# Expert weights fetched by SyncE at a row held in a register, instead of by a GpSimd gather

## What is computed

```python
logits = x @ router_w + router_b
topk_scores, topk_idx = top_k(logits, 2)          # 2 of 8 experts for each token
gates = softmax(topk_scores)
for e in range(8):                                # D_MODEL 256, D_FF 1024
    h = relu(x @ W1[e] + b1[e])
    y = h @ W2[e] + b2[e]
    out += y * combine[..., e]                    # the gate of expert e, 0 where it was not chosen
```

## Time and profile before

| | us |
|---|---|
| median of 3 runs | 1067.77 (1062.13 to 1068.28) |
| the profiled execution | 1060.41 |
| its span in the profile | 1058.5 |
| first block, up to the barrier | about 369 |
| expert stage, first tile's loads to last scatter | about 369 to 1058.5 |

### The profile page before, as it was taken

How to read it: one execution, slowest core, us unless ns; L and a number is a source line. 1 busy time by engine, 2 the same in 40 slices (tenths; PEclk the granted TensorE clock), 3 DMA queues, 4 the chain that set the end, 5 groups by cost and what they waited for, 6 DMA issues and landing times. The chain is left out here.

```text
span 1058.5 us, 19059 instructions
## 1 busy us (share of the span) xinstructions
PE 909.3 (86%) x5742; PEld 769.5 (73%) x5742; DVE 801.6 (76%) x2058; ACT 608.9 (58%) x1166; POOL 552.6 (52%) x461
## 2 busy tenths in 40 slices
PE   4788887888754059999999999999999999999994
PEld 3456565555533049988988998998998998999893
DVE  1799999999993357787787787777777778778761
ACT  2798888888871035564554564555556545556441
POOL 0104665646464353575575566467557457457424
PEclk9999999999985569999999999999999999999997
DMA  8342534433111064565564466457447456556423
GB/s 264 120 149 91 169 102 139 129 120 89 37 54 45 16 220 176 125 146 141 164 161 139 121 199 157 114 141 207 126 127 209 129 122 163 180 125 146 125 26 40
DMA packets 71671, 138.97 MB, mean 131 GB/s; under 512 B 10925, under 2 KB 62766, under 8 KB 67658
## 3 DMA queue, kind: packets, MB, share of 16 engines
q0 software_dynamic: 31136, 98.34, 35.2%
q1 hardware_dynamic: 40490, 40.08, 12.3%
HBM read 110.52 MB, written 27.86 MB: 131 GB/s over the span
## 5 line engine op out<-in xcount | busy, mean ns | idle before, releaser
L1055 ACT ACTIVATE hid<-hp,b 128x512 f32<-128x512 f32 (+1 forms) x248 | 158.6, 639 | 303.0 <-PE hp L1090 297.8
L1102 PE MATMUL acc<-whi,hhi 128*128 128x256 f32 x880 | 246.0, 280 | 0.0
L1102 PE MATMUL acc<-whi,hlo 128*128 128x256 f32 x880 | 245.9, 279 | 0.0
L1102 PE MATMUL acc<-wlo,hhi 128*128 128x256 f32 x880 | 245.3, 279 | 0.0
L1186 DVE CAST hhi<-hid 128x512 fp32r<-128x512 f32 (+1 forms) x248 | 107.2, 432 | 148.1 <-ACT hid L1055 147.4
L1017 POOL DMA_INDIRECT out_rows<-yout,dest x110 | 179.8, 1634 | 63.9 <-issue 45.8
L1090 PE MATMUL hp<-xhi,whi 128*128 128x512 f32 (+1 forms) x496 | 187.6, 378 | 10.0 <-DVE xlo L1133 7.7
L341 POOL DMA_INDIRECT expert_lists<-tid,slots x96 | 134.0, 1396 | 113.1 <-DVE cand L736 56.3
L1090 PE MATMUL hp<-xlo,whi 128*128 128x512 f32 (+1 forms) x496 | 183.8, 371 | 0.0
L1090 PE MATMUL hp<-xhi,wlo 128*128 128x512 f32 (+1 forms) x496 | 183.6, 370 | 0.0
L1031 ACT ACTIVATE whi<-raw 128x512 fp32r<-128x512 f32 x248 | 154.3, 624 | 41.3 <-DMA raw<-in_ew,idx 41.3
(11 more groups left out here) (185 smaller groups left out, 1442.2 us busy)
## 6 DMA issues: line engine op xcount, KB each, us to landing
xin<-in_x SPq DMA_DIRECT2D x32, 512.0 KB
xin<-in_x SPq DMA_DIRECT2D x32, 256.0 KB
token_rows<-xs SPq DMA_DIRECT2D x16, 388.5 KB, 3.9
out_rows<-h SPq DMA_DIRECT2D x16, 384.0 KB, 2.6
xg<-token_rows,tid POOLq DMA_INDIRECT x110, 2.9
out_rows<-yout,dest POOLq DMA_INDIRECT x110, 4.1
expert_lists<-tid,slots POOLq DMA_INDIRECT x96, 5.3
out_rows<-zrow SPq DMA_DIRECT2D x1, 512.0 KB
```

Source lines behind the costliest of these rows:

```text
L1055: act.activation(hid[:, c % 2, 0:j.r * P], hp[c % 2][:, 0:j.r * P], ACT.Relu, bias=b1[:, j.s, c:c + 1]).then_inc(hid_done, 1)
L1102: last = pe.matmul(acc_of(j, r), h_[:, c % 4, r * P:(r + 1) * P], w_[:, j.s, at:at + C], start=c == 0 and n == 0 and r % 2 == 0, stop=c == ...
```

## The change

The weights are no longer gathered by POOL. `gather_w` and its calls go, and with them POOL's two waits that guarded the slot of `raw` (`wlo_done`, `b1_done`). A block for SP is new: it waits for `idx` of the tile, reads the first row's number from partition 0 of `idx` into a register (`value_load`) and issues one plain DMA of 128 rows of `ew` from there, on SP's queue. It does so for the first two tiles at the start, and in the body of j for tile a, as soon as the slot is free and `idx` of a is there.

```diff
@@ def first() of gpsimd
                 pool.wait_ge(idx_ready, 1)
                 gather_tid(T0)
-                gather_w(T0)
                 gather_x(T0)
                 pool.wait_ge(idx_ready, 2)
                 gather_tid(T0.nxt())
                 gather_b2(T0)
-                gather_w(T0.nxt())
                 gather_x(T0.nxt())
@@ def body(j) of gpsimd
                 if a.exists():
                     pool.wait_ge(idx_ready, a.at(1, 1))
-                    pool.wait_ge(wlo_done, j.at(FC, FC))
-                    pool.wait_ge(b1_done, j.at(1, 1))
                     pool.wait_ge(marks, j.at(N_MARK, N_MARK))
                     pool.wait_ge(x_in[j.s], j.rows_in_slot(j.r))
                     end_of_waits()
-                    gather_w(a)
                     gather_tid(a)
@@ new
+        @block.sync
+        def _(sp):
+            def fetch_w(j):
+                sp.wait_ge(idx_ready, j.at(1, 1))
+                end_of_waits()
+                row = sp.value_load(idx[0:1, j.i, 0:1], min_val=0, max_val=(E - 1) * P)
+                sp.dma_start(raw[:, j.s, :], ew[bass.ds(row, P), :]).then_inc(w_in[j.s], 16)
+
+            def first():
+                fetch_w(T0)
+                fetch_w(T0.nxt())
+
+            def body(j):
+                a = j.after()
+                if a.exists():
+                    sp.wait_ge(wlo_done, j.at(FC, FC))
+                    end_of_waits()
+                    sp.wait_ge(b1_done, j.at(1, 1))
+                    end_of_waits()
+                    fetch_w(a)
+
+            tiles(sp, first, body)
```

More of the change, by code:

```diff
@@ L935, in experts @@
         xt = [ps("xt0"), ps("xt1")]
-        idx_ready, waits_over = sem("idx_ready"), sem("waits_over")
+        idx_ready, waits_over, sp_waits_over = sem("idx_ready"), sem("waits_over"), sem("sp_waits_over")
         w_in, tid_in, x_in, b2_in, y_sent = ([sem(f"{n}{s}") for s in range(2)] for n in ("w_in", "tid_in", "x_in", "b2_in", "y_sent"))
@@ L959, in end_of_waits @@
                 pool.sem_inc(waits_over, 1)
-            def gather_w(j):
-                pool.indirect_dma_start(raw[:, j.s, :], None, ew, bass.IndirectOffsetOnAxis(idx[:, j.i, 0:1], 0)).then_inc(w_in[j.s], 16)
             def gather_tid(j):
@@ L1022, in _, with end_of_waits @@
             pool.wait_ge(y_sent[LAST.s], LAST.rows_in_slot(LAST.r))
+        @block.sync
+        def _(sp):
+            def end_of_waits():
+                sp.sem_inc(sp_waits_over, 1)
+            def fetch_w(j):
[15 more added lines that the diff above has]
+            tiles(sp, first, body)
         @block.scalar
```

## The result

| | before | after |
|---|---|---|
| median of 4 runs | 1066.61 us (1062.13 to 1068.28) | 1119.11 us (1114.52 to 1120.20) |
| ratio | 1 | 1.049, 95% interval 1.045 to 1.054 |
| span of the profiled execution | 1058.5 us | 1117.4 us |

The changed kernel is 4.9% slower. The direction was as forecast, the size was not: 52.5 us against the 38 forecast, and 1119.1 lies just above the range (1066 to 1118).

A forecast was written before the change was run, and what follows sets the result against it. PE was taken as the limit (608.67 of 620 us in the expert stage's body). Collision 27.3, clock 7.5 and start 3.0 sum to 38 us slower, from 1065 to 1103 us, range 1066 to 1118.

The forecast's parts named there:

- POOL's relief: Expert stage: 31 weight issues leave POOL, 1.45 us sooner at its wait for `ysum`; gain taken as 0, bound 1 us.
- SP's path: SP, idle until then: wait, register load taken as 0.5 us, register operations, one DMA; issue 0.6 us after `idx`.
- The collision after a half tile: Last `xg` gather, which PE awaits, meets 2.1 MB of weights: 3.9 us late, seven times, 27.3 us (0 to 35).
- the scatter that came 3.0 us late: `expert_lists` scatter at 180.6, SP's loads filling the other queue: landed after 7.8 us, 3.8 to 4.8 when quiet.
- The clock: PE after a gap: 3 us at half clock, 1.5 us lost, in five of seven gaps; 7.5 us, bounds 0 and 10.5.
- The start: Start of expert stage: `tid` and the first gathers stand behind the first weights; 3 us later, or 1.5 faster if queues share.
- Fair shares: Rival, chance 0.20: queues alternate row by row, gather about 1.3 us late seven times, no clock loss; 1074 us.
- Late weights: Rival, chance 0.16: SP's load and issue take 1.2 us more, weights flow after the gather, nothing changes; 1064 us.
- Faster: Rival, chance 0.06: freed POOL brings the gather before PE, DVE's gap shrinks; up to 11.3 us, 1.5 at start; 1052 us.

The follow-up runs named there:

- tiny_w: The changed kernel, with SP fetching only 32 columns of each weight row from the third tile on; 1068.32 us, 1.008 of before.
- pool_less: The kernel of before, with POOL gathering the weights of the first two tiles alone and nobody those of the others; 1064.53 us, 1.003 of before.
- late: The changed kernel, with SP issuing the weights of the tile after next only once the next tile's token rows have landed; 1068.68 us, 1.007 of before.
- half_w: The changed kernel, with SP fetching only the first half of each weight row from the third tile on; 1089.25 us, 1.026 of before.
- start: The changed kernel, with the first weights issued after the first tile's `tid` landed, the second after its token rows; 1112.95 us, 1.050 of before.
- late_start: The kernel of late, with first weights issued after the first tile's `tid` landed, the second after its token rows; 1066.08 us, 1.005 of before.
- late_pool2b: The kernel of late, with the weights of the first two tiles gathered by POOL as before; 1062.89 us, 1.002 of before.
- x_first: The kernel of before, with POOL gathering token rows before scattering results in the body of a half tile; 1055.73 us, 0.9956 of before.
- quarters: The changed kernel, with the weights in four DMAs of a quarter of the columns each; 1103.99 us, 1.040 of before.

## Why the prediction was right in its course and too small

**POOL's relief is worth nothing** (the removed part): held. `b2s` starts 0.82 us after `ysum` in both kernels, and tiny_w and pool_less show it without the collision.

**SP's path** (the added part): held. The register load, of which before had no row, took 0.28 us, its register operations 0.16; from `idx` to the DMA it was 0.82 us, where I had 0.6. In the changed kernel (duration in ns, min/median/max):

```profile
L1025 SPq TENSOR_LOAD <-idx x31: 270/276/461, 372.1 to 1026.7; - x31
L1025 SPq FUSED_REGOPS  x31: 152/152/172, 372.6 to 1027.0; - x31
```

The Trainium skill's floor of about 0.6 us for a `tensor_load` ("DMA: Bandwidth & Descriptors", Latency and other measured facts) is not what these rows show, 0.27 to 0.46 us from SBUF on SP.

**The collision after a half tile** (the moved part): the mechanism held and is shown by late, half_w and tiny_w. Its size was taken too low. I had put 3.9 us between the scatter that came 3.0 us late and a gather behind the whole stream, 4.8. Measured: 4.7 in the mean, the upper end. One thing in the mechanism was not as I had put it: the gather's bytes did not come behind the whole stream but from 54 to 61% of its time on (in six of the seven places), among the later rows; the completion that PE waits for came at about the stream's end, 854.48 and 854.44 us. The scatter was a poor neighbour: the loads in its way moved in rows of about 1 KB, those in the gather's way in rows of 16 KB. The term was too small by 5.8 us.

**The clock**: this is the step that failed, the largest miss, 8.1 us. I had read 3 us at half clock from one row, 1.5 us lost, in five of seven gaps: 7.5 us, with 10.5 as the bound. It came in all seven, in four of them the stretch was twice as long, and PE worked 4.6 us in the mean at half clock behind a gap: 15.6 us in all, some 0.7 of them in the first tile. That is beyond the bound. The row I had taken was right, but one row doesn't give a length.

**The start**: 3.6 us where I had 3.0, and `tid` waited as described. start and late_start confirm the order of the queues for half of it only; late_pool2b, with all of the first loads on POOL's queue again, has no late start.

**Not in the sum at all**: the last DRAIN, 3.6 us, a consequence of the change that I could not have read in the trace of before; and the barrier, 3.0 us, which differs from run to run and belongs to neither kernel. 37.8 + 5.8 + 8.1 + 0.6 + 3.6 + 3.0 = 58.9.

**The rivals.** Fair shares (1074): falls for one transfer of 2.1 MB. A turn after each row of weights would have given gaps of 1.3 us more; they were 4.7, and even with the weights in four DMAs 3.1. The Trainium skill ("DMA: Bandwidth & Descriptors", Queues, rings and completion order) has an engine empty a whole packet of one queue, typically some 9 to 17 descriptors, before it goes to the next, which is not a turn after each row. The trace agrees in so far as 66 rows of weights passed without one of the gather. Late weights (1064): SP was 0.2 us slower than taken, not 1.2. Faster (1052): the point at which it decides, `b2s` sooner than 0.82 us after `ysum`, was never reached.

## What to carry to other kernels

A transfer taken off a queue loses the order that the queue gave it: before moving a large prefetch to another queue, look for the small transfer that some engine waits for with no slack, and see whether the prefetch will now overtake it. A wait on that transfer's semaphore before the prefetch is issued gives the order back (4.9% here against 0.7%). And where an engine waits for a queue's last transfer, order on the queue is worth trying before load: x_first won 0.44%, 0.3% of it in the gaps, by moving the scatters behind the gathers.

## What the runs showed of the hardware that I had not expected

- A gather of 128 rows of 1,036 bytes, landed and seen by PE 3.0 us after its issue when alone, took 7.6 us behind a 2.1 MB load that another engine had issued 0.26 us ahead on another queue. Its packets moved from 4.8 us after the issue on and not from 1.8, behind some 60% of the load and not behind all of it. The gap of PE was, in the median, 5.0, 2.6 and 0.4 us behind rows of 16,416, 8,208 and 128 bytes.
- PE's seven gaps of 4.9 to 5.8 us were each followed by TensorE at 1.2 GHz, for 3.3 to 5.9 us after its restart; it cost some 15 us beside the 33.1 of the gaps. In quarters it came behind all seven gaps of 2.6 to 4.3 us. In half_w it came behind the gap of 5.0 us and three of the five of 2.5 to 2.6, and not behind the one of 3.2. Gaps of up to 1.2 us had it in no trace.
- POOL's DRAIN at the end of the program took 2.68, 5.53 and 6.43 us with 0, 29 and 31 fewer DMAs issued by POOL, whatever SP did, and 3.09 us with all of them in another order (x_first). The cause is open.
